# A first chunk loaded during the attention, the base rows on ScalarE and a first search with no chunks beside it, in a four-image vision block

## The reference, cut to what matters

```python
h = h + attention(layernorm(h))            # 'base' plus the projection of attention_out
x = layernorm(h)
weights = x @ wr + br                      # one gate per token
_, idx = top_k(weights, 1568); sel_idx = idx[:, :1567]     # per image
y = gelu(x[sel_idx] @ w1 + b1) @ w2 + b2
processed = zeros.at[sel_idx].set(y * weights[sel_idx])
out = h + (processed + x)
```

## Time and profile before

| | |
|---|---|
| median of three runs | 6038.59 us |
| the profiled execution's own time | 6045.59 us |
| its span, first to last instruction | 6043.7 us |
| PE, DVE, ACT, POOL busy | 96%, 72%, 54%, 73% of the span |
| last stage | 5407.7 us to the end |

### The profile page before, as it was taken

One profiled execution on the slowest core, in us unless ns is written; L12 is line 12 of the kernel. 1 busy time (PEld: TensorE's weight loads), 2 busy tenths in 40 slices (PEclk: granted clock), 3 DMA queues, 4 the chain that ended last, 5 costly groups with the idle time before them and its releaser, 6 DMA issues. The chain is left out here.

```text
span 6043.7 us, 121186 instructions
## 1 busy us (share of the span) xinstructions
PE 5792.6 (96%) x37698; PEld 3439.8 (57%) x37698; DVE 4375.8 (72%) x8484; ACT 3267.4 (54%) x6740; POOL 4386.4 (73%) x1475
## 2 busy tenths in 40 slices
PE   5999998999999999999999999999999999974899
PEld 4777776555555555555555555555555555533566
DVE  4777776877777777777777777777777777726630
ACT  2545554366666665666666566666666666641222
POOL 2444444588888888888888888888888888874452
PEclk9999999799999999999999999999999999987999
DMA  2323325111011111101111110111111000024442
GB/s 68 103 95 101 100 95 154 37 39 37 18 37 35 29 27 39 39 20 40 36 30 28 40 39 19 40 36 30 28 39 39 19 20 20 16 57 149 114 94 38
DMA packets 197574, 308.62 MB, mean 51 GB/s; under 512 B 38038, under 2 KB 162334, under 8 KB 193998
## 3 DMA queue, kind: packets, MB, share of 16 engines
q1 hardware_dynamic: 181958, 280.23, 16.6%
q0 software_dynamic: 12432, 19.38, 1.6%
q10 hardware_dynamic: 2680, 2.63, 0.1%
HBM read 178.45 MB, written 124.50 MB: 50 GB/s over the span
## 5 line engine op out<-in xcount | busy, mean ns | idle before, releaser
L1346 DVE TENSOR_REDUCE tops<-ps_m 128x1 f32<-128x448 f32 x5600 | 3110.1, 616 | 877.0 <-PE ps_m L1249 844.9
L1322 ACT ACTIVATE prob<-ps_s 128x448 f32<-128x448 f32 (+1 forms) x5600 | 2606.5, 548 | 1715.1 <-PE ps_s L1185 1697.5
L1155 POOL TENSOR_TENSOR tile_sum<-prob 128x1792 f32<-128x1792 f32 x448 | 1803.1, 4025 | 616.4 <-ACT prob L1322 615.8
L1185 PE MATMUL ps_s<-queries,keys 97*128 97x448 f32 (+1 forms) x5600 | 2202.6, 397 | 12.7 <-ACT prob L1322 6.9
L1249 PE MATMUL ps_m<-keys,queries 96*128 96x448 f32 x5600 | 2091.1, 379 | 11.9 <-POOL ident_r L1133 9.2
L1155 POOL TENSOR_TENSOR tile_sum<-tile_sum,prob 128x1792 f32<-128x1792 f32 x448 | 1808.1, 4036 | 32.6 <-ACT prob L1322 0.9
L1185 PEld LDWEIGHTS ps_s<-queries,keys 97*128 97x128 f32 (+1 forms) x5600 | 1044.1, 187 | 1151.3 <-ACT prob L1322 647.7
L1201 PE MATMUL ps_o<-prob,values 128*32 128x448 f32 x11200 | 1345.0, 552 | 0.2 <-ACT prob L1322 0.2
L1249 PEld LDWEIGHTS ps_m<-keys,queries 96*128 96x128 f32 x5600 | 1061.5, 190 | 205.8 <-DVE tops L1346 74.5
L1201 PEld LDWEIGHTS ps_o<-prob,values 128*32 128x32 f32 x11200 | 226.2, 108 | 377.2 <-issue 247.4
L1213 PE MATMUL ps_d<-tile_sum,ones 128*32 128x448 f32 x3584 | 423.8, 545 | 3.0 <-POOL tile_sum L1155 3.0
(11 more groups left out here) (181 smaller groups left out, 4133.6 us busy)
## 6 DMA issues: line engine op xcount, KB each, us to landing
queries<-q_parts SPq DMA_DIRECT2D x288, 192.0 KB, 4.0
keys<-k_parts SPq DMA_DIRECT2D x96, 392.0 KB, 7.5
xT<-in_x SPq DMA_DIRECT2D x56, 224.0 KB, 2.6
hidden_and_bias<-base SPq DMA_DIRECT2D x28, 448.0 KB, 3.1
q_parts<-hi SPq DMA_DIRECT2D x56, 224.0 KB, 1.9
q_parts<-lo SPq DMA_DIRECT2D x56, 224.0 KB, 1.9
k_parts<-hi SPq DMA_DIRECT2D x56, 224.0 KB, 1.9
k_parts<-lo SPq DMA_DIRECT2D x56, 224.0 KB, 1.9
```

The lines of the kernel that those rows point to most:

```text
L1155: nc.gpsimd.tensor_tensor(tile_sum[k % 2][:, :, :], left, prob[:, t % SLOTS, :, :], ALU.add).then_inc(summed, 1)
L1185: mm = nc.tensor.matmul(o[:, 0:CH], keys[x.u][:, j, at:at + k], queries[x.v][:, j, own:own + CH], start=True, stop=not last, skip_group_ch ...
L1322: nc.scalar.activation(prob[0:k, t % SLOTS, j, :], ps_s[0:k, score_bank(x.hm, i), 0:CH], ACT.Exp).then_inc(exp_done, 1)
L1346: nc.vector.tensor_reduce(tops[0:rows, j, r - blocks[0], c:c + 1], ps_m[0:rows, e % MB, 0:CH], AX.X, ALU.max).then_inc(m_used, 1)
```

## The change

1. A class `LastStage` holds the tile `values0` of the attention, allocated for both blocks. In the attention's last phase that tile is not used, and parts of it are `w_proj`, `w_gate`, `aT` of chunk 0 and `base` of chunk 0. SP loads them in the third half of that phase. In the last stage SP starts with the loads of chunks 1 to 3, and b_gate comes behind them with a semaphore of its own, `gate_in`, for which DVE waits at its start.
2. `base` has tiles of its own (four, beside four of `h`): DVE's `hidden` reads `base` and writes `h`. SP loads `aT` and `base` two spots after a chunk, ahead of the store, and w_up, w_down, b_up and b_down only at spot 17.
3. `add_base` moves from POOL to ACT. It is now four ACTIVATE operations, h * (rstd + 1) + off, behind the four of `norm`; DVE makes `grown` = rstd + 1 beside `off`. `norm` and `add_base` come 2 spots after the chunk, `gates` 3.
4. Eight chunks start at spots 0 to 14; the first image's search has spots 16 to 28 with one step each and no chunk; six more chunks start at 29 to 39 beside its scatters, three per spot, at 29 to 38. `AROUND` is 41. The other 14 chunks start at 41 and every third spot. The second, third and fourth search end 3, 4 and 4 spots later than before, counted from `AROUND`.

```diff
+class LastStage:
+        self.values = ctx.enter_context(nc.sbuf_tensor("values0", [128, KT, HG * DH], F32))
+        self.w_proj = part(128, CT, C)
+        self.w_gate = part(QT, 1, C)
+        self.aT = part(128, G, CH)
+        self.base = part(QT, NQ, C)
...
+            def load_last_stage():
+                sp.dma_start(last_stage.w_proj, ...).then_inc(last_stage.proj_in, 16)
+                sp.dma_start(last_stage.w_gate[:, 0, :], ...).then_inc(last_stage.proj_in, 16)
+                for v in range(2):
+                    sp.wait_ge(out_out[v], ONE + 16 * PER_IMAGE)
+                for g in range(G):
+                    sp.dma_start(last_stage.aT[:, g, :], d.a2[g]).then_inc(last_stage.a_in, 16)
+                sp.dma_start(last_stage.base, d.base[0]).then_inc(last_stage.base_in, 16)
...
                     shifts(y, 0)
+                    if last_phase(x) and x.s == 2:
+                        load_last_stage()
...
-AROUND = 33
+FIRST_CHUNKS, MORE_CHUNKS = 8, 6
+SEARCH_SPOTS = 13
+AROUND = 2 * (FIRST_CHUNKS + MORE_CHUNKS) + SEARCH_SPOTS
-CHUNK_AT = [2 * m for m in range(16)] + [AROUND + 3 * k for k in range(CHUNKS - 16)]
-SCALE_BEHIND, NORM_BEHIND, BASE_BEHIND, GATE_BEHIND = 2, 3, 4, 5
+CHUNK_AT = [2 * m + (SEARCH_SPOTS if m >= FIRST_CHUNKS else 0) for m in range(FIRST_CHUNKS + MORE_CHUNKS)]
+CHUNK_AT += [AROUND + 3 * k for k in range(CHUNKS - len(CHUNK_AT))]
+SCALE_BEHIND, NORM_BEHIND, BASE_BEHIND, GATE_BEHIND = 2, 2, 3, 3
...
-            spot += i % (4 if b == 0 else 3) == 0
+            spot += i % 3 == 0
...
-            for m in range(loaded):
-                load(m)
-            sp.dma_start(w_up[:, :, :], ...)          # and w_down, b_up, b_down
+            for m in range(1, BASE_TILES):
+                if m < AT_TILES:
+                    load_a(m)
+                load_base(m)
+            sp.dma_start(b_gate[:, :], ...).then_inc(gate_in, 16)
             for x in range(END):
+                if x == SEARCH_AFTER[0] + 2:
+                    sp.dma_start(w_up[:, :, :], ...)  # and w_down, b_up, b_down
+                if x - 2 in chunk_at and chunk_at[x - 2] + AT_TILES < CHUNKS:
+                    load_a(chunk_at[x - 2] + AT_TILES)
+                if x - 2 in chunk_at and chunk_at[x - 2] + BASE_TILES < CHUNKS:
+                    load_base(chunk_at[x - 2] + BASE_TILES)
+                if x - 1 - BASE_BEHIND in chunk_at:
+                    store(chunk_at[x - 1 - BASE_BEHIND])
...
             def root(m):
                 pool.wait_ge(veps_ready, m + 1)
                 if m >= 2:
                     pool.wait_ge(xn_ready, NQ * (m - 1))
+                    pool.wait_ge(off_ready, 2 * (m - 1))
-            def add_base(m):                                         # POOL
-                nc.gpsimd.tensor_tensor(h[m % 4][:, :, :], h[m % 4][:, :, :], pay[:, at:at + NQ, 0:C],
-                                        ALU.add).then_inc(base_ready, 1)
+            def add_base(m):                                         # ACT
+                act.wait_ge(xn_ready, NQ * (m + 1))
+                for r in range(NQ):
+                    ins = nc.scalar.activation(h[m % H_TILES][:, r, :], h[m % H_TILES][:, r, :], ACT.Identity, bias=off[m % 2][:, r:r + 1],
+                                               scale=grown[m % 2][:, r:r + 1])
+                ins.then_inc(base_ready, 1)
...
-            dve.wait_ge(proj_in, 16 * 3)
+            dve.wait_ge(proj_in, 32)
+            dve.wait_ge(gate_in, 16)
...
+                added = base[m % BASE_TILES][:, 2 * a:2 * a + 2, :].rearrange("p r c -> p (r c)")
+                nc.vector.tensor_tensor(rows, ps_p[0:QT, a, :], added, ALU.add).then_inc(p_kept, 1)
...
+                nc.vector.tensor_scalar(grown[m % 2][:, :], rstd[m % 2][:, :], 1.0, None, ALU.add).then_inc(off_ready, 1)
```

More of the change, by code:

```diff
@@ L1476, in gated_ffn @@
         gate = sb("gate", [QT, B, TILES])
-        w_proj = sb("w_proj", [128, CT, C])
-        w_gate = sb("w_gate", [QT, C])
+        w_proj = last_stage.w_proj
+        w_gate = last_stage.w_gate[:, 0, :]
         b_gate = sb("b_gate", [QT, 1])
         minus_half = sb("minus_half4", [QT, NQ])
-        aT = [sb(f"aT4{i}", [128, G, CH]) for i in range(3)]
-        h = [sb(f"h4{i}", [QT, NQ, C]) for i in range(4)]
+        aT = [last_stage.aT] + [sb(f"aT4{i}", [128, G, CH]) for i in range(1, AT_TILES)]
+        base = [last_stage.base] + [sb(f"base4{i}", [QT, NQ, C]) for i in range(1, BASE_TILES)]
+        h = [sb(f"h4{i}", [QT, NQ, C]) for i in range(H_TILES)]
         stats = sb("stats4", [QT, NQ, 6])
@@ L1487, in gated_ffn @@
         rstd = [sb(f"rstd4{i}", [QT, NQ]) for i in range(2)]
-        off = [sb(f"off{i}", [QT, NQ]) for i in range(2)]
+        off, grown = ([sb(f"{n}{i}", [QT, NQ]) for i in range(2)] for n in ("off", "grown"))
         product = sb("product", [QT, NQ, C])
@@ L1528, in gated_ffn @@
         tables_set = sem("tables_set")
-        a_in = [sem(f"a_in4{i}") for i in range(3)]
-        h_in = [sem(f"h_in4{i}") for i in range(4)]
+        gate_in = sem("gate_in")
+        a_in = [last_stage.a_in] + [sem(f"a_in4{i}") for i in range(1, AT_TILES)]
+        base_in = [last_stage.base_in] + [sem(f"base_in{i}") for i in range(1, BASE_TILES)]
         p_ready, p_kept = sem("p_ready"), sem("p_kept")
@@ L1535, in gated_ffn @@
         base_ready, dots_ready, gate_ready = sem("base_ready"), sem("dots_ready"), sem("gate_ready")
-        base_out = [sem(f"base_out{i}") for i in range(4)]
+        base_out = [sem(f"base_out{i}") for i in range(H_TILES)]
         step, counted, slots_ready = sem("step"), sem("counted"), sem("slots_ready")
@@ L1556, in _, with load_a, load_base @@
         def _(sp):
[L1557 to L1563, removed]
-                for g in range(G):
[L1565 to L1568, removed]
+            def load_a(m):
+                if m >= AT_TILES:
+                    sp.wait_ge(p_ready, 2 * (m - AT_TILES) + 2)
+                for g in range(G):
+                    sp.dma_start(aT[m % AT_TILES][:, g, :], d.a2[2 * m + g]).then_inc(a_in[m % AT_TILES], 16)
+            def load_base(m):
+                if m >= BASE_TILES:
+                    sp.wait_ge(p_kept, 2 * (m - BASE_TILES) + 2)
+                sp.dma_start(base[m % BASE_TILES][:, :, :], d.base[m]).then_inc(base_in[m % BASE_TILES], 16)
             def store(m):
                 sp.wait_ge(base_ready, m + 1)
-                sp.dma_start(d.out[m].rearrange("(i p) c -> p i c", p=QT), h[m % 4][:, :, :]).then_inc(base_out[m % 4], 16)
+                sp.dma_start(d.out[m].rearrange("(i p) c -> p i c", p=QT), h[m % H_TILES][:, :, :]).then_inc(base_out[m % H_TILES], 16)
             def load_rows(u):
@@ L1597, in _ @@
                 for u in load_at.get(x, []):
                     load_rows(u)
-            for i in range(4):
-                sp.wait_ge(base_out[i], 16 * (CHUNKS // 4))
+            for i in range(H_TILES):
+                sp.wait_ge(base_out[i], 16 * len(range(i, CHUNKS, H_TILES)))
             for i in range(2):
```

88 lines of the change are left out of this document (48 added, 40 removed).

## The result

The kernel after takes 6019.76 us (median of ten runs, 6016.26 to 6025.52), beside 6039.83 us (6034.76 to 6049.87) for the kernel before on the same chip. The ratio is 0.9968, 95% interval 0.9960 to 0.9977: faster, by 20.1 us where 30.4 were forecast. The profiled execution took 6016.26 us (span 6014.5), against 6045.59; 8.0 of these 29.3 us lie ahead of the last stage.

A forecast was written before the change was run, and what follows sets the result against it. Between the attention's end and the first unit, PE was not taken as the bound: POOL, DVE and the DMA take turns. Parts A to C saved 40.4 us, part D cost 10; 30.4 off 6038.59 gave 6008.2 us, range 5993 to 6023.

The forecast's parts named there:

- the forecast case: Whole kernel: 30.4 us shorter, 6008.2 us, with its own range 6001 to 6016; chance 0.62.
- Part A: Last stage's start to first tally: DVE waits for b_gate, then eight chunks at 5.3 us; gain 11.8 us.
- Part B: First image's search, tally to slots: 34.2 us without chunks between its steps, instead of 53.6; gain 19.4 us.
- Part C: Slots to the first unit's turn: POOL's scatters and roots bound it, 48.6 us instead of 57.85; gain 9.2 us.
- Part D: The units, with 14 chunks beside them instead of 12: 10 us longer, bounds +3 and +25.
- Tally wait and the cold clock behind it: In the units: PE's 5.8 us wait for a tally and 2 us of cold clock after it go.
- Unit 3: At unit 3's turn: PE stalls about 4 us for the second image's rows, whose search and scatters end later.
- The fourth image: In the units: the fourth image's rows, four spots later, cost 1 us.
- Gelus: In the units: ACT's norm and add_base make gelus late by 0.5 to 1 us, six times; 5 us.
- The rival with late rows: At unit 3: stall of 12 to 15 us as POOL waits for each root's variance; 6018.6 us, chance 0.12.
- The cold stretch: First eight chunks: PE at 1.2 GHz, 7.2 us each, or the DMA at 230 GB/s; 6021.6 us, chance 0.09.
- The slower rival: Beside the units: ACT's norm and add_base before gelus hold PE at every chunk; up to 6062 us, chance 0.04.

The follow-up runs named there:

- the two later profiles: Both kernels profiled once more, unaltered: the kernel after, 6005.98 us, ratio 0.9961 to the kernel before; and the kernel before, one run of 6025.05 us.

## Why the prediction was right up to the first turn, and 11.6 us off

The measured 6019.76 us lies inside the range of 5993 to 6023, but outside the 6001 to 6016 that the forecast case gave itself; it stands nearest to the 6018.6 and 6021.6 of two rivals. Of the 11.6 us, 9.2 are in the last stage (parts A to C 2.8 better, part D 12 worse), 1.2 are the median of the kernel before, which came out at 6039.83, and 1.1 are between the difference of the medians (20.1) and that of the two profiled stages (21.2). That the sum stayed inside the range is in part luck: the largest cost of the measured kernel, the hold, stands in none of its terms and none of its rivals.

- **Part A (11.8 us; measured 12.9, and 12.7 between the two later profiles).** Right in its steps: b_gate is what DVE waits for, 5.28 us a chunk, the early load worth nothing. Moving that one transfer brought 6.9 us. The Trainium skill (DMA: Bandwidth & Descriptors, Queues, rings and completion order) has descriptors consumed in ring order on each DMA engine; the trace agrees, with 8.3 us from issue to landing behind the seven transfers, 3.6 to 4.3 behind two, and 2.7 with nothing ahead of it in the stage. That `aT` was late was the main reason for 6.5 us a chunk before; POOL's add beside DVE cost under 1 us there, for of the additions of 112x8 ahead of the tally one took 1.11 us and the others 0.17.
- **Part B (19.4; measured 19.5).** 34.3 us in every profile with these spots and without POOL's adds.
- **Part C (9.2; measured 10.7, and 10.6).** POOL's bound was right; with its adds back the stretch takes 54.9 and 55.6 us.
- **Part D (+10 with bounds 3 and 25; measured +22, and +18.0 without the hold).** This term was mis-sized. Against the two later profiles, step by step: two more chunks at the forecast's 7 (PE's busy time on `ps_p` alone grew by 5.8). Tally wait and the cold clock behind it −8, then +2 for the new tally wait: measured −4.0 together (5.7 to 1.7), and the clock didn't come back, PE being busy 3.6 us more than the chunks explain. Before, the granted clock fell behind the tally's wait (0.71 in 5682.3 to 5697.3); after, it falls behind unit 9's stall instead (0.77 in 5886.6 to 5901.6). So the forecast's −6 came out at −0.4, the largest miss of the sum; that the 3.6 us are the clock's is argued, not shown. Unit 3: 2.97 (forecast 4). The fourth image: 5.28 at unit 9's turn, where I had put 1; this is the second step that failed, for I gave it a number without working out its slack as I had for unit 3. Gelus: 7.4 (forecast 5), with 1.6 less for xT. Counts: 2.5 less. That makes 18. In the first profile the stalls for rows are nearly absent (0.73 us at unit 3, none at unit 9) and the hold stands in their place.
- **The base of the sum.** I subtracted 30.4 from an execution in which the hold was already present. On that chip it grew: PE has idle times of 3.48 and 13.87 us in it after, against 6 us in all before (busy 44.0 us in the 50 from 5860). Over the whole of the units that is 4 us: 22.0 given back in the first pair of profiles, 18.0 in the second. The hold isn't a property of the change, but what it costs depends on where PE stands when it comes.

Stage against stage of the two later profiles the change is worth 25.3 us, and by medians on their chips 23.2; the forecast of 30.4 is 5 to 7 too high: part D took 8 more, and the parts before it gave 3 more. The rival with late rows, taken at 12 to 15 us for unit 3, had the right kind of event at the wrong unit and half the size. The cold stretch was short: a chunk's two halves take 3.68 us from the fourth chunk on, from the fifth in the second profile. The slower rival named ACT: 7.4 us, against 35.4 needed. But one of the signs of being wrong, ACT as PE's releaser for more than 15 us after the first unit, did come in the first profile of the kernel after (14.6, 9.8 and 0.8 us, 25.2 in all); without the hold it is 8.9 us.

The add on ACT was costed for POOL's time alone. Its other worth, up to 9 us at the tally by the two runs with POOL's adds (+65.3 and +57.6 beside +56.3), stands in no step: POOL's add and DVE's addition with two operands in SBUF exclude each other. The Trainium skill (SBUF — State Buffer, Who interferes with whom) says that the pair of ports that DVE and GpSimd share is an exclusive lock; the trace agrees, with 0.17 us for the instruction where no add of POOL's is under way, and 0.76 and 1.73 us where one is, ending with it. The kernel before escaped it for 24 of its 28 chunks by waiting for the next offset before its add; in the other four the addition took 0.52, 1.11, 1.70 and 1.89 us.

## What to carry to other kernels

A transfer that the first instruction of an engine waits for belongs ahead of the bulk on its queue, however small it is: its place here was worth 6.9 us at the tally, and all the preloading 5.4. Work taken out of a serial stretch reappears beside the dense one (26 us saved, 20 given back), so count for each item that has slack there how many spots it loses, to the last of them. And before a reference execution is used as a base, look whether its longest idle times have a releaser that the kernel explains.

## What was not expected of the hardware

- The hold. It is in all five profiles taken where the kernel before takes 6038.6 to 6040.2 us, and in none of the eight from the two chips on which it takes 6026.8 to 6029.2. There ACT takes up a finished product of PE up to 18 us late, and DVE one 13 us late (the profile after), beside an unbroken run of 31 to 34 indirect DMAs of POOL; the same run on the other chips holds nobody up. In each of the five, ACT's last long wait ends 2.6 to 3.4 us after POOL's run has ended. That it is a matter of the chip is read from these thirteen profiles; what happens in it stays open, and breaking up the run of scatters wasn't tried.
- The DVE addition of 112x8 that takes 0.17 us alone and 1.73 us beside POOL's 2.17 us add (3.32 once, beside the units, ending with a POOL add there too), at a place where shifting and holding the add decides over 7.7 us.
